# The order of a GpSimd queue: four row sends of a batch, moved and split over the steps of an attention

## The reference

```
x = x + L0_attn(norm(x)); x = x + L0_ffn(norm(x))      # linear attention; int8 weights
x = x + L1_attn(norm(x)); x = x + L1_ffn(norm(x))      # causal attention; grouped top-4 of 16 experts
x = x + L2_attn(norm(x)); x = x + L2_ffn(norm(x))      # gated delta rule; ternary weights
x = x + L3_attn(norm(x)); x = x + L3_ffn(norm(x))      # below; top-2 of 8 experts
```

```
probs = softmax(flat @ Wg); topp, topi = top_k(probs, 2)
for e in range(8):
    h = silu(flat @ W1[e]) * (flat @ W3[e])
    out = out + cw[:, e:e+1] * (h @ W2[e])
```

## Time and profile before

| what | value |
| --- | --- |
| median of three runs | 2025.56 us (2020.61 to 2027.13) |
| the profiled execution, its own time | 2014.69 us |
| its span, first to last instruction | 2012.9 us |
| mean granted TensorE clock | 0.879 of full speed |
| TensorE matmul, busy | 1589.8 us (79%) |
| VectorE, busy | 1136.1 us (56%) |
| ScalarE, busy | 843.5 us (42%) |
| GpSimd, busy | 564.3 us (28%) |

### The profile page before, as it was taken

The page is one execution under the profiler, slowest core; times in us unless marked ns, Lnnn a source line. Parts: engine busy times, 40 slices in busy tenths (PEclk is TensorE's granted clock), DMA queues, the critical chain, the costliest instruction groups (busy, mean ns, idle before and its releaser), DMA issues. The chain is left out here.

```text
span 2012.9 us, 46758 instructions
## 1 busy us (share of the span) xinstructions
PE 1589.8 (79%) x16783; PEld 1167.5 (58%) x16783; DVE 1136.1 (56%) x3048; ACT 843.5 (42%) x1634; POOL 564.3 (28%) x782
## 2 busy tenths in 40 slices
PE   4788999999488879699987776888887588353992
PEld 3655666666256647478875554555554488242882
DVE  5745677777445448356644576876674343552434
ACT  2422455555211115334432344655554476001763
POOL 4111011111101103422212211133233355374554
PEclk9989899999699989799997987998897799555996
DMA  4000222221099200000001002222220242221224
GB/s 173 1 2 10 65 57 61 55 55 44 8 286 328 91 0 1 1 3 3 3 3 64 1 1 58 66 68 66 64 71 21 64 113 86 71 74 45 78 78 144
DMA packets 84684, 124.99 MB, mean 62 GB/s; under 512 B 17329, under 2 KB 70577, under 8 KB 82929
## 3 DMA queue, kind: packets, MB, share of 16 engines
q1 hardware_dynamic: 75824, 104.30, 17.8%
q0 software_dynamic: 8640, 17.78, 2.5%
HBM read 67.47 MB, written 55.59 MB: 61 GB/s over the span
## 5 line engine op out<-in xcount | busy, mean ns | idle before, releaser
L1527 DVE TENSOR_REDUCE small<-ps 128x8 f32<-128x1024 f32 (+1 forms) x256 | 312.5, 1223 | 120.8 <-PE ps L1313 70.4
L1454 ACT ACTIVATE scr<-ps 128x1024 f32<-128x1024 f32 x256 | 262.0, 1023 | 239.7 <-PE ps L1288 121.2
L244 POOL TENSOR_TENSOR rstd<-vare,neghalf 128x4 f32<-128x4 f32 (+1 forms) x72 | 63.2, 878 | 543.6 <-DVE vare L223 542.2
L2826 POOL DMA_INDIRECT results<-scr x142 | 135.9, 957 | 143.8 <-DVE scr L2815 59.3
L1326 PE MATMUL ps<-scr 128*32 128x256 f32 x2048 | 174.0, 414 | 0.2 <-ACT scr L1454 0.2
L1275 PEld LDWEIGHTS ps<-scr_r 32*128 32x128 f32 x1024 | 82.3, 195 | 156.0 <-ACT scr L1454 88.8
L1275 PE MATMUL ps<-scr_r 32*128 32x256 f32 x1024 | 136.3, 344 | 35.8 <-ACT scr L1454 21.8
L2746 PE MATMUL ps<-scr 128*128 128x128 f32 x1136 | 153.4, 279 | 1.3 <-ACT scr L2773 1.3
L1306 PE MATMUL ps<-scr_r 32*128 32x256 f32 x1024 | 137.8, 351 | 10.0 <-DMA scr_r<-scr_r 5.5
L2746 PEld LDWEIGHTS ps<-scr 128*128 128x128 f32 x1136 | 141.9, 196 | 1.6 <-issue 1.6
L1911 PE MATMUL ps<-scr 64*64 64x64 f32 x4480 | 120.0, 223 | 13.3 <-DVE scr L2201 7.1
(11 more groups left out here) (410 smaller groups left out, 3547.7 us busy)
## 6 DMA issues: line engine op xcount, KB each, us to landing
scr_r<-scr_r SPq DMA_DIRECT2D x512, 64.0 KB
rows_m<-kinds SPq DMA_DIRECT2D x8, 2064.0 KB, 30.2
rows_f<-kinds SPq DMA_DIRECT2D x8, 2064.0 KB, 74.7
scr<-results SPq DMA_DIRECT2D x32, 256.0 KB
scr<-rows_m SPq DMA_DIRECT2D x71, 64.5 KB
scr<-rows_f SPq DMA_DIRECT2D x71, 64.5 KB
scr<-in_l3m SPq DMA_DIRECT2D x1, 3072.0 KB, 11.1
results<-scr POOLq DMA_INDIRECT x142
```

What stands on the lines that cost most here:

```text
L244: pool.tensor_tensor(k.rstd[:, 0:self.J], k.vare[:, 0:self.J], k.neghalf[:, 0:self.J], ALU.pow).then_inc(self.e["rstd_ready"].sem, 1)
L1454: act.activation(PT[:, g % 2, 2 * x:2 * x + 2, :], ps[:, 4:6, :], ACT.Exp).then_inc(e["prob_ready"].sem, 1)
L1527: dve.tensor_reduce(nf[:, half, 0:blocks, at:at + 2].rearrange("p q a -> p a q"), ps[:, 2 * (p % 2):2 * (p % 2) + 2, :].rearrange("p a (q ...
L2826: pool.indirect_dma_start(results, bass.IndirectOffsetOnAxis(ap=names[:, j % IN, P:P + 1], axis=0), y[:, j % OUT, :], None).then_inc(store ...
```

## The change

On GpSimd, `send_in(b, s, t)` sends one tile t after waiting for `st_ready(b, s + 1)`, the signal that the turned scores of step s are done. Tiles 0 and 1 stay between `combined(b, 1)` and `combined(b + 1, 0)`, with the waits of steps 1 and 2 ahead of them; tiles 2 and 3 go behind `ln.pool_rstd(b - 1)`, with the waits of steps 6 and 7. In the round of b = 16 there is no such wait. The three rounds behind the loop are as they were.

```diff
+        def send_in(b, s, t):
+
+            if has(b):
+                pool.wait_ge(e["st_ready"].sem, e["st_ready"].at(b, s + 1))
+            sort.send(pool, b // 2 - 2, b % 2, range(t, t + 1))
+
@@
                 sort.name(pool, b // 2 - 2, b % 2)
-                sort.send(pool, b // 2 - 2, b % 2, range(2))
+                send_in(b, 1, 0)
+                send_in(b, 2, 1)
             if has(b + 1):
                 combined(b + 1, 0)
-            if sort and b >= 4:
-                sort.send(pool, b // 2 - 2, b % 2, range(2, 4))
             if has(b - 1):
                 ln.pool_rstd(pool, b - 1)
                 if ln.natural is None:
                     ln.pool_keep(pool, b - 1)
+            if sort and b >= 4:
+                send_in(b, 6, 2)
+                send_in(b, 7, 3)
```

## The result

The changed kernel takes 2002.14 us (median of four runs, 1993.32 to 2007.38); before, with one more run beside it, 2023.17 (2020.61 to 2027.13). The ratio is 0.9886 [0.9856, 0.9915], so it is faster, by about 23 us (21.0 between the medians); the forecast was 10.8 us too slow (2012.9). The profiled executions stand 21.4 us apart: 2014.69 before, 1993.32 after (span 1991.5, mean granted clock 0.890 for 0.879). Each is faster than the median of its kernel, by 10.9 and 8.8 us; the repeat under the experiments shows an execution nearer the median of the change.

What follows compares the result with a forecast made beforehand. ScalarE's exponentials, waiting for TensorE's signals while sends run, were taken to pace the attention. -16 - 10 + 12.1 + 1.2 = -12.7 us, from 2025.56 to 2012.9 us; range 2001 to 2032 over all cases.

Steps and rivals of the forecast that it cites:

- Step 6, -16 and -10: Attention batches 4 to 14: freeing step 6 of sends saves 16 us of waits, and 10 us more go with them.
- the rest of 10: Remainder of the 26.0 us lost in batches 4 to 14, put down to matmuls at 1.2 GHz: -10 us.
- Tiles 2 and 3 in step 7: GpSimd's queue: these tiles go back to back behind 1/sqrt at the start of step 7, not alone.
- no hold in step 7: Rival: the pair sent in step 7 delays nothing, with queues nearly empty; -24.8 us, 2000.8 us, chance 0.12.
- The new hold, +12.1: Wait before the next batch's step 0, behind tiles 2 and 3: 1.13 us in even batches, 1.07 in odd, +12.1 us.
- the 0.4 for the ranking: Odd batches, step 7: ranking's signal falls between the sends, making VectorE's places and TensorE's transposes late by 0.4 us.
- Tiles 0 and 1, cost 0: Steps 1 and 2: waiting for each step's scores and sending each tile alone costs 0 us.
- The tail, +1.2: Round of b = 16: tiles 2 and 3 behind batch 15's 1/sqrt make the next name late, +1.2 us.
- The reading of the hold: Attention steps: a send holds TensorE's signals to ScalarE while SyncE's head copies are under way; 2.73 us idle in batch 8.
- not the sends: Rival: step 6 waits come from something else recurring there, so only the added tail cost remains; 2026.8 us, chance 0.11.
- The slower case (2032.5): Rival: the pair in step 7 delays step 0 by 1.7 us (even) or 2.3 (odd), clock low; +6.9 us, chance 0.18.
- the case of 2022.9: Rival: the clock stays low in the attention batches, so only direct waits count; -2.7 us, 2022.9 us, chance 0.17.

Runs made afterwards that it cites:

- the repeat: The changed kernel measured once more, nothing altered: 2001.28 us, ratio 0.9874 against the kernel before.
- the order alone: Kernel before with only tiles 2 and 3 moved behind 1/sqrt, no wait added, tiles 0 and 1 still a pair: 2002.45 us, ratio 0.9865.

## Why the prediction was off

**Step 6, -16 and -10: right in direction, the parts not so sharp.** Both together are the 26.0 us lost over the pace without sends. The waits in front of step 6 are 0.85 or 0.86 in every batch. From step 5 to step 7 the eleven batches had lost 13.5 us against batches 2 and 3, not 16. The clock of the stretch is 1.00 in the execution shown, but 0.94 in the repeat and 0.95 with the order alone, for 0.88 before: the rest of 10 went wholly in one execution and in part in the others. The times do not show that it needed the split of tiles 0 and 1: the order alone has the same ratio within the noise.

**Tiles 2 and 3 in step 7: right.** A pair, right behind 1/sqrt, 1.35 us apart. The case "no hold in step 7", 2000.8, came nearest in number, but its mechanism did not occur.

**The new hold, +12.1: the failed term.** In front of step 0 it measured 6.7 us in all, and by the marks only 5.0 us are left of all losses. The step was "If the hold is the one of batch 8, it ends 0.63 us after the send". In step 7 of even batches the hold ended with the second send (0.02 us after it in batch 8): 2.38 from step 7 to step 0 for 1.90, 0.48 us and not 1.13, and 0.20 in batch 14. Odd batches lost 0.65 to 0.94, where I had 1.07; there the hold outlasts its send by 0.61 to 0.90 us, the 0.63 of the row or more, and nothing is seen of the 0.4 for the ranking. That is 2.57 in the even and 4.17 in the odd batches, 6.7 us. Of it 1.0 is caught up behind it: from step 0 to step 1 batches 6, 8, 10, 12 and 14 then take 1.85, where batch 4, without a hold, takes 2.05. I had named 0 and 21.7 as the bounds, and took the offset of batch 8 although no row showed a pair in step 7. Why the offset is 0 behind even batches and 0.6 and more behind odd ones is open; the copies begin beside the pair in both.

**Tiles 0 and 1, cost 0: wrong in two batches.** They went as a pair in step 2 of batches 9 and 11 and held step 3, 1.0 and 0.4 us.

**The tail, +1.2: right up to the name, wrong in sum.** From the start of the last 1/sqrt to the name of the second round behind the loop it was 9.53 us (1555.36 to 1564.89) and is 10.82:

```profile
1527.72 0.72 POOL L244 TENSOR_TENSOR rstd<-vare,neghalf 128x2 f32<-128x2 f32 x1 [4.89 <-DVE vare L223]
...
1538.54 0.21 POOL L2628 COPY XT<-xn 128x4 int32<-128x4 int32 x1
1540.86 0.98 POOL L2642 DMA_INDIRECT rows_m<-XT,small  x1 [2.11 <-issue]
```

Another 1.3 us came behind it, 1.0 of it in front of the first send after this name (idle 2.11 us, 1.12 before); for what it waited is open. So the tail cost 2.6 us. But from the mark of batch 15 to the end of the last send it was 53.5 us (1525.03 to 1578.52 before) and is 50.5: batch 15 itself was 5.7 us shorter up to the last 1/sqrt, with a mean clock of 0.61 from 1525 to 1556 us before and 0.85 from 1503 to 1528 us after, and my sum stopped at its mark. From step 3 on, four steps took 3.2, 2.8, 3.3 and 2.3 us before and 1.9 after. I counted eleven batches where twelve gained.

**The reading of the hold: half right.** That sends in flight make ScalarE wait for TensorE is shown from both sides: take them off the signal and the wait goes, put other GpSimd work there and none comes. TensorE's work was done: in batch 8 of the kernel before its scores of step 6 end, by its records, at 1400.32, and ScalarE starts at 1402.24.

```profile
1399.81 0.28 PE L1306 MATMUL ps<-scr_r 32*128 32x256 f32 x2
1399.92 0.40 PE L1281 MATMUL ps<-scr_r 32*128 32x256 f32 x4
```

```profile
1401.49 1.23 DVE L1527 TENSOR_REDUCE small<-ps 128x4 f32<-128x1024 f32 x1
```

VectorE, which waits for the signal of L1306, started 0.75 us before ScalarE, though the two signals are, by the records, 0.2 us apart. So whether TensorE's signal leaves late or ScalarE alone sees it late is not shown. Nor is which signal: in front of the even steps the exponential also waits for TensorE's product with the values of the step before (`pv_done`, L1326), and the profile names only the scores. That copies under way are the condition is refuted: with them the wait is mostly 0.8 to 0.9 us longer, and with a pair and no copy it is 1.9. What the pair of the earlier trace rows shows stays open: a signal seen by ScalarE in the midst of a send.

**The case "not the sends"** is refuted with it. The Trainium skill, SBUF — State Buffer, "Who interferes with whom", says that a DMA never contends with a compute engine. The runs agree for the bytes (1/32 of them brought no gain), and that section speaks of memory ports. But indirect DMAs issued on GpSimd made ScalarE wait 1.9 to 2.9 us for TensorE's signal, where it waits 0.86; the measurement decides.

The slower case (2032.5) needed a mean hold of 1.35 us in front of step 0; it was 6.7 / 11 = 0.6. The clock came back, wholly or in part, against the case of 2022.9.

How eight earlier transfers lengthen a hold by 0.9 us when their bytes do not matter is not settled; four or six of them were not tried, nor eight that are all issued well before the pair. Eight are not enough by themselves: in the kernel before, batches 5, 11 and 13 have them too and wait only 2.15, 1.96 and 1.92 us in front of step 6.

## What to carry over

An indirect DMA that GpSimd issues costs more than its microsecond on GpSimd: here ScalarE often saw a signal of TensorE raised meanwhile only when the row of sends was nearly or wholly over. Placing a send right behind such a signal, so that it ends before the next, and never two in a row across one, took all these waits away. In the kernel before, the holds of step 6 cost 13.5 of the 26.0 us directly, and much of the rest went with them as the clock rose from 0.88 to between 0.94 and 1.00; with waits of 1.9 us it was 0.96. So look at the granted clock by stretch before pricing a stall, and in more than one execution. And when a cost is carried to a new place, ask which of the conditions of its row hold there; here the offset did not.

## What was not expected of the hardware

In front of step 6, one send across the signal made ScalarE wait 1.3 to 1.5 us, a pair without copies 1.9, a pair behind eight copies mostly 2.7 to 3.1 (1.9 to 2.3 in the rest), whether they were of 64 KB or of 2. GpSimd's arithmetic of 2.26 us across it made none. TensorE's matmul time in the same 2120 instructions was 190.04 us at a mean granted clock of 0.89 and 168.94 at 1.00.
